# A graph network on one core: the decoder's first layer in split passes of 512 nodes, and a new order of edge blocks 0 and 1

## The reference

```python
m = gelu(h_E @ m0_w + m0_b)              # h_E: 16384 x 512, m: 16384 x 256
m = gelu(m @ m1_w + m1_b)
m = gelu(m @ m2_w + m2_b)
dh = segment_sum(m, src, 512) / 30
h = layer_norm(h_V + dh, ln1_g, ln1_b)
d = gelu(h @ d0_w + d0_b)                # the decoder: 256 -> 1024
d = gelu(d @ d1_w + d1_b)                # 1024 -> 1024
h = layer_norm(h + d @ d2_w + d2_b, ln2_g, ln2_b)
```

## Time and profile before

| | before |
|---|---|
| median of 3 runs | 592.72 us (591.55 to 592.8) |
| the profiled execution, its own time | 591.97 us |
| its span, first to last instruction | 590.1 us |
| TensorE busy | 574.3 us, 97% of the span |
| VectorE, ScalarE, GpSimd busy | 462.4, 368.9, 225.0 us |

### The profile page before, as it was taken

One profiled execution on the slowest core, in us unless ns is written; L12 is line 12 of the kernel. 1 busy time (PEld: TensorE's weight loads), 2 busy tenths in 40 slices (PEclk: granted clock), 3 DMA queues, 4 the chain that ended last, 5 costly groups with the idle time before them and its releaser, 6 DMA issues.

```text
span 590.1 us, 8593 instructions
## 1 busy us (share of the span) xinstructions
PE 574.3 (97%) x3032; PEld 487.5 (83%) x3032; DVE 462.4 (78%) x791; ACT 368.9 (63%) x564; POOL 225.0 (38%) x211
## 2 busy tenths in 40 slices
PE   7989999999999999999999999999999999999995
PEld 6778888888888888888888888888888889677763
DVE  5986487878778887788998889879766566898767
ACT  6866686767778777777776678767366444211242
POOL 4075577556666543555544555530000000200111
PEclk9999999999999999999999999999999999999999
DMA  8255487295567628456553875333163304000001
GB/s 289 87 199 168 145 284 221 115 290 177 167 187 227 190 94 260 154 153 215 163 186 110 315 247 178 114 91 88 49 271 122 142 11 143 0 2 0 1 0 36
DMA packets 34504, 86.86 MB, mean 147 GB/s; under 512 B 3872, under 2 KB 23200, under 8 KB 29856
## 3 DMA queue, kind: packets, MB, share of 16 engines
q1 hardware_dynamic: 27264, 67.09, 36.3%
q0 software_dynamic: 6912, 19.10, 8.6%
q10 hardware_dynamic: 288, 0.13, 0.1%
HBM read 66.69 MB, written 19.62 MB: 146 GB/s over the span
## 4 chain that ended last, share of the span: by engine, by line
PE 84%; DVE 9%; ACT 2%; issue 2%; POOL 1%; DMA 1%; POOLq 0%; ACTq 0%
PE ps L1356 27%; PE ps L1408 10%; PE ps L1566 7%; PE ps L1414 5%; PE ps L1390 5%; PE ps L1451 5%; PE ps L1386 5%; PE ps L1385 4%; PE ps L1528 4%; PE ps L1607 2%; PE ps L1453 2%; PE ps L1663 1%; PE ps L1578 1%; PE ps L1597 1%; PE ps L1480 1%
## 5 line engine op out<-in xcount | busy, mean ns | idle before, releaser
L497 POOL DMA_INDIRECT sorted_rows<-m,place x120 | 166.9, 1391 | 151.7 <-ACT m L560 123.7
L543 ACT ACTIVATE m_hi<-ps,cols 128x512 fp32r<-128x512 f32 x128 | 88.6, 692 | 66.8 <-PE ps L1356 41.6
L877 DVE TENSOR_TENSOR m_lo<-m_out,m_hi 128x512 fp32r<-128x512 f32 x128 | 88.6, 694 | 50.9 <-ACT m_out L545 48.0
L1356 PE MATMUL ps<-x_hi,w_hi 128*128 128x512 f32 x248 | 97.1, 391 | 0.5 <-DVE x_lo L751 0.5
L1356 PE MATMUL ps<-x_lo,w_hi 128*128 128x512 f32 x248 | 97.0, 391 | 0.0
L1356 PE MATMUL ps<-x_hi,w_lo 128*128 128x512 f32 x248 | 96.7, 390 | 0.0
L545 ACT ACTIVATE m_out<-ps,cols 128x512 f32<-128x512 f32 x128 | 88.5, 691 | 1.7 <-DVE m_lo L877 1.7
L751 DVE TENSOR_TENSOR x_lo<-x_raw,x_hi 128x1024 fp32r<-128x1024 f32 x62 | 73.1, 1219 | 5.3 <-ACT x_hi L537 5.3
L1408 PE MATMUL ps<-w_lo,m_hi 128*128 128x256 f32 x256 | 64.2, 283 | 0.0
L1408 PE MATMUL ps<-w_hi,m_hi 128*128 128x256 f32 x256 | 64.0, 282 | 0.0
L560 ACT ACTIVATE m<-m_in 128x512 f32<-128x512 f32 x64 | 39.5, 635 | 38.0 <-DVE m_in L890 38.0
(11 more groups left out here) (231 smaller groups left out, 1137.1 us busy)
## 6 DMA issues: line engine op xcount, KB each, us to landing
x_raw<-in_edges_dram SPq DMA_DIRECT2D x31, 1024.0 KB, 6.2
sorted_raw<-sorted_rows SPq DMA_DIRECT2D x24, 647.5 KB, 4.7
sorted_raw<-sorted_rows SPq DMA_DIRECT2D x6, 518.0 KB, 4.1
d_w<-in_d_dram SPq DMA_DIRECT2D x3, 1024.0 KB, 8.9
d_w<-in_d_dram SPq DMA_DIRECT2D x1, 3072.0 KB, 10.0
rows<-in_rows_dram SPq DMA_DIRECT2D x1, 2176.0 KB, 10.1
sorted_rows<-m,place POOLq DMA_INDIRECT x120, 4.8
w_raw<-in_w_dram SPq DMA_DIRECT2D x4, 256.0 KB, 5.8
```

What stands on the lines that cost most here:

```text
L497: pool.indirect_dma_start(out=sorted_d, out_offset=bass.IndirectOffsetOnAxis(ap=place[:, at:at + 1], axis=0), in_=m2[:, b % 2, t], in_offs ...
L543: nc.scalar.activation(out_hi[:, m], ps[:, bank], ACT.Gelu, bias=col(bias, m)).then_inc(hi_signal, 1)
L877: nc.vector.tensor_tensor(lo[:, m], m_out[:, m], hi[:, m].bitcast(F32), ALU.subtract).then_inc(done, 1)
L1356: last = nc.tensor.matmul(out, left, right, start=(k == 0 and i == 0), stop=(k == KE - 1 and i == 2))
```

## The change

**Edge stage.** `keep_warm` ahead of the first layer issues 7 products and not 10. `layer_0_first` takes both output halves (m = 0, 1) of a pass before the next pass, waits for high parts first and for low parts only ahead of the third pass. `layer_0(1, 0)` does the two passes with the high part of the input for all four k, then the third pass. On VectorE `rest_1(1, 0)` and `rest_1(1, 1)` go ahead of `rest_x(3)`.

**Decoder.** `d0_w` is split (`d0w_hi` by ScalarE, `d0w_lo` by VectorE, in the place of `d0_w`), and so are its inputs (`first_hi` by ScalarE from the turned columns, `first_lo` by VectorE in `first_rest`, which recomputes the plain value). There are 11 units: m = 0 to 2 for each half of 256 nodes, m = 3 to 7 for all 512. Third passes of the first and of the second three units come together, behind filler products. `d2_w` is loaded ahead of the GRU's weights.

**GRU.** For the last chunk the products of `w_hh` come before those of `w_ih`, into a bank of their own (`LAST_IN`), and VectorE's first candidate step waits for them alone.

```diff
@@ -252,7 +268,12 @@
...
         GRU_BANKS = (0, 4, 6, 0)
+        LAST_IN = 2
         NODE_HALF = (range(0, NC // 2), range(NC // 2, NC))
+        D0_HALVED = 3
+        D0_UNITS = ([(m, slice(half * N // 2, (half + 1) * N // 2)) for half in range(2) for m in range(D0_HALVED)]
+                    + [(m, slice(0, N)) for m in range(D0_HALVED, KD)])
+        UNITS = len(D0_UNITS)
...
@@ -433,10 +457,10 @@
...
             sp.dma_start(d1_w[:, D1_FIRST:].rearrange("p a b -> p (a b)"), d1_d[:, D1_FIRST * D:]).then_inc(d1_loaded, 16)
+            sp.wait_ge(d0_done, UNITS)
+            sp.dma_start(d2_w, d2_d.rearrange("p (a b) -> p a b", b=H)).then_inc(d2_loaded, 16)
...
                 sp.dma_start(dst[:].rearrange("p a b -> p (a b)"), src).then_inc(gru_loaded, 16)
-            sp.wait_ge(d0_done, 2 * KD)
-            sp.dma_start(d2_w, d2_d.rearrange("p (a b) -> p a b", b=H)).then_inc(d2_loaded, 16)
...
@@ -633,6 +657,8 @@
...
                 round_sorted(q)
+            act.wait_ge(early_loaded, 48)
+            nc.scalar.activation(d0w_hi[:], d0_w[:], ACT.Copy).then_inc(d0w_hi_done, 1)
...
@@ -663,21 +689,27 @@
...
-            act.wait_ge(early_loaded, 48)
-            affine(0, "ln1_g", "ln1_b")
+            def first_columns(half):
...
+                turned[0] += 1
+                act.wait_ge(hat_turned, turned[0])
+                for k in range(KH):
+                    nc.scalar.activation(first_hi[:, k, HALF[half]], turned_bank(half, k), ACT.Identity,
+                                         bias=col("ln1_b", k), scale=col("ln1_g", k)).then_inc(first_hi_done, 1)
...
+            first_columns(0)
             counts_out(COUNTS - 1)
-            for i in range(2 * KD):
-                half, m = divmod(i, KD)
+            for i, (m, nodes) in enumerate(D0_UNITS):
                 if i == 2:
-                    affine(1, "ln1_g", "ln1_b")
-                if i in (8, 11):
+                    first_columns(1)
+                if i in (7, 9):
                     act.wait_ge(d1_loaded, 16)
-                    round_d1w(i // 11)
+                    round_d1w(i // 9)
                 act.wait_ge(d0_done, i + 1)
-                gelu_split_out(i, ps[:, D0_BANK[m % 4], 0:NH], col("d0_b", m), d0_hi[:, m, HALF[half]])
+                gelu_split_out(i, ps[:, D0_BANK[i % 4], 0:nodes.stop - nodes.start], col("d0_b", m), d0_hi[:, m, nodes])
...
                 act.wait_ge(d1_done, m + 1)
-                gelu_split_out(2 * KD + m, ps[:, D1_BANK[m % 4]], col("d1_b", m), d1_hi[:, m])
+                gelu_split_out(UNITS + m, ps[:, D1_BANK[m % 4]], col("d1_b", m), d1_hi[:, m])
...
@@ -966,18 +998,23 @@
...
                 q = b - LAG_PREP
+                if b == 1:
+                    rest_1(1, 0)
+                    rest_1(1, 1)
...
                         add_counts(s, (b - first) // 2, (b - first) % 2)
-                rest_1(b, 0)
+                if b != 1:
+                    rest_1(b, 0)
...
                     hot_dst(q, 0)
-                rest_1(b, 1)
+                if b != 1:
+                    rest_1(b, 1)
...
@@ -1030,6 +1067,8 @@
...
             rest_direct(DIRECT[1], 1)
+            dve.wait_ge(d0w_hi_done, 1)
+            nc.vector.tensor_tensor(d0w_lo[:], d0_w[:], d0w_hi[:].bitcast(F32), ALU.subtract).then_inc(d0w_split, 1)
...
@@ -1107,6 +1146,17 @@
...
+            def first_rest(half):
...
+                dve.wait_ge(first_hi_done, KH * (half + 1))
+                for k in range(KH):
+                    nc.vector.tensor_scalar(act_T[:, k, HALF[half]], turned_bank(half, k), col("ln1_g", k), col("ln1_b", k),
+                                            ALU.mult, ALU.add).then_inc(first_plain, 1)
+                dve.wait_ge(first_plain, KH * (half + 1))
+                part = (slice(None), slice(None), HALF[half])
+                nc.vector.tensor_tensor(first_lo[part], act_T[part], first_hi[part].bitcast(F32),
+                                        ALU.subtract).then_inc(first_split, 1)
...
@@ -1127,19 +1177,23 @@
...
                 link(last)
-                moments(NODE_HALF[half])
+                variance(NODE_HALF[half])
+                if half:
+                    first_rest(0)
+                dve.wait_ge(rstd_ready, norms[0])
                 hats_written(half, lambda c: normed(res, hat, c))
-            for i in range(2 * KD):
-                half, m = divmod(i, KD)
-                rest_gelu(i, NH, d0_hi[:, m, HALF[half]], d0_lo[:, m, HALF[half]])
-                if i in (10, 12):
-                    rest_d1w(i // 12)
-                if i in (3, 5, 7, 13):
-                    piece = (3, 5, 7, 13).index(i)
+            for i, (m, nodes) in enumerate(D0_UNITS):
+                rest_gelu(i, nodes.stop - nodes.start, d0_hi[:, m, nodes], d0_lo[:, m, nodes])
+                if i == 0:
+                    first_rest(1)
+                if i in (7, 9):
+                    rest_d1w(i // 9)
+                if i in (2, 4, 5, 8):
+                    piece = (2, 4, 5, 8).index(i)
...
             for m in range(KD):
-                rest_gelu(2 * KD + m, N, d1_hi[:, m], d1_lo[:, m])
+                rest_gelu(UNITS + m, N, d1_hi[:, m], d1_lo[:, m])
...
@@ -1308,10 +1362,16 @@
...
+                bank = GRU_BANKS[c] + 1
+                hidden, inputs = ps[:, bank, H:2 * H], ps[:, bank, 0:H]
+                if c == NC - 1:
+                    hidden, inputs = ps[:, bank, 0:H], ps[:, LAST_IN, 0:H]
+                    dve.wait_ge(last_hidden, 1)
+                else:
+                    dve.wait_ge(gru_done, c + 1)
+                link(nc.vector.tensor_tensor(cand[:, c], hidden, rz[:, c, 0:H], ALU.mult))
                 dve.wait_ge(gru_done, c + 1)
-                bank = GRU_BANKS[c] + 1
-                link(nc.vector.tensor_tensor(cand[:, c], ps[:, bank, H:2 * H], rz[:, c, 0:H], ALU.mult))
-                nc.vector.tensor_tensor(cand[:, c], cand[:, c], ps[:, bank, 0:H], ALU.add).then_inc(cand_ready, 1)
+                nc.vector.tensor_tensor(cand[:, c], cand[:, c], inputs, ALU.add).then_inc(cand_ready, 1)
...
@@ -1348,6 +1408,18 @@
...
                 out = ps[:, (1, bank_x(b - 1))[m]]
+                if b == 1 and m == 0:
+                    for k in range(KE):
+                        if k % 2 == 0:
+                            pe.wait_ge(x_hi_done, 2 * b + k // 2 + 1)
+                        for part in (w_hi, w_lo):
+                            nc.tensor.matmul(out, w(0, k, m, part), x_hi[:, 1, k], start=(k == 0 and part is w_hi), stop=False)
+                    for k in range(KE):
+                        if k % 2 == 0:
+                            pe.wait_ge(x_lo_done, 2 * b + k // 2 + 1)
+                        last = nc.tensor.matmul(out, w(0, k, m, w_hi), x_lo[:, 1, k], start=False, stop=(k == KE - 1))
+                    last.then_inc(l0_done, 1)
+                    return
...
@@ -1480,7 +1560,7 @@
...
             pe.wait_ge(ident_ready, 1)
-            keep_warm(10, 0)
+            keep_warm(7, 0)
...
@@ -1518,7 +1598,7 @@
...
                 acts[0] += KH
-                return acts[0]
+                return acts[0] - 2 * KH
...
@@ -1541,37 +1621,53 @@
...
             keep_warm(2, 0)
-            turned = [turn_rows(hat, 0), None]
+            turn_rows(hat, 0)
             keep_warm(4, 0)
-            for i in range(2 * KD):
-                half, m = divmod(i, KD)
+            pe.wait_ge(d0w_split, 1)
+            for i, (m, nodes) in enumerate(D0_UNITS):
                 if i == 2:
-                    turned[1] = turn_rows(hat, 1)
-                if m == 0:
-                    pe.wait_ge(act_ready, turned[half])
+                    turn_rows(hat, 1)
...
                     pe.wait_ge(gelu_out, i - 3)
-                to_columns(d0_w, KH, m, act_T, half, ps[:, D0_BANK[m % 4], 0:NH]).then_inc(d0_done, 1)
+                out = ps[:, D0_BANK[i % 4], 0:nodes.stop - nodes.start]
+                for part in (d0w_hi, d0w_lo):
+                    for k in range(KH):
+                        if part is d0w_hi and i in (0, D0_HALVED):
+                            pe.wait_ge(first_hi_done, KH * (i // D0_HALVED) + k + 1)
+                        nc.tensor.matmul(out, part[:, k, m * P:(m + 1) * P], first_hi[:, k, nodes],
+                                         start=(k == 0 and part is d0w_hi), stop=False)
+                if i < 2 * D0_HALVED and i % D0_HALVED < D0_HALVED - 1:
+                    continue
+                if i < 2 * D0_HALVED:
+                    keep_warm(2 if i < D0_HALVED else 4, 7 if i < D0_HALVED else 2)
+                    pe.wait_ge(first_split, i // D0_HALVED + 1)
+                for u in range(i - D0_HALVED + 1 if i < 2 * D0_HALVED else i, i + 1):
+                    part_m, part_nodes = D0_UNITS[u]
+                    out = ps[:, D0_BANK[u % 4], 0:part_nodes.stop - part_nodes.start]
+                    for k in range(KH):
```

(63 more changed lines are left out.)

## The result

| | before | after |
|---|---|---|
| median of 12 runs each | 592.22 us (591.51 to 592.9) | 592.95 us (592.17 to 595.14) |
| the profiled execution | 591.97 us, span 590.1 | 592.93 us, span 591.1 |

The ratio is 1.0016, 95% interval [1.0009, 1.0024]: slower by some 0.9 us. That is clear of the noise, but even the upper end is barely over 0.2%. The forecast was 592.9. One execution of run 6 (638.08 us, mean granted clock 0.851) and one of run 7 (718.21 us, 0.753) ran in a slower state of the chip: they are in those two medians (591.42 and 592.66 us without them) and in no ratio. Two parts of the change pull against each other, and the profile has each at its place.

A forecast was written before the change was run, and what follows sets the result against it. TensorE was taken as the bound, carrying 84% of the chain of waits. Opening and block 1 -2.14, decoder +2.3 and last chunk +0.05 sum to +0.2 us, 592.9 us on the median; range 589.5 to 594.5.

The forecast's parts named there:

- The total: Whole kernel: the three terms sum to +0.2 us, giving 592.9 us on the median.
- two pauses in the decoder: Decoder's first layer: TensorE waits 1.2 us for hat of half 1 and 1.7 us for the columns of half 1.
- The opening: First microseconds: seven fillers instead of ten bring layer 1 of block 0 from 13.56 to 13.2, 0.35 us.
- Block 1: Low parts come earlier on VectorE, removing TensorE's 1.54 us wait and 0.25 restart; -2.14 us together with the opening.
- Rival 2: Block 1: VectorE stays behind, two biased and rest_0(2, 0) arriving after 36.96; 594.0 us, chance 0.12.
- The decoder: Decoder's first layer: queue-order waits and d1w_split make D1 start at 450.3 instead of 448.00, +2.3 us.
- D1 some 16.5 us after the first product: Decoder, a sign to look for: D1 starts 16.5 us after the decoder's first product instead of 14.2.
- Rival 1: Decoder: TensorE stays the bound and neither pause is seen; decoder -0.9, time 589.7 us, chance 0.34.
- my bound of -0.9: Decoder's first layer, lower bound of its term: TensorE never waits and D1 starts at 447.1.
- Rival 3: Decoder: the clock falls, products at half rate cost about 1.5 us more; 594.4 us, chance 0.08.
- the row of block 1: Block 1 before: a 1.54 us pause at granted clock 1.00, read as showing the decoder's pauses wouldn't slow the clock.

The follow-up runs named there:

- run 6: Changed kernel with the decoder's transposes of half 1 moved behind fillers and third passes of units 0 to 2: 591.44 us, ratio 0.9985 to the kernel before.
- run 7: Changed kernel with more filler products ahead of the transposes and of unit 3, so TensorE never rests in the decoder's pauses: 592.69 us, ratio 1.0010 to before.
- run 1: Kernel before with the edge stage's part alone (opening and VectorE's order in block 1): 590.10 us, ratio 0.9962.
- run 8: Changed kernel without the 12 filler records inside the decoder's units: 592.77 us, ratio 1.0006 to the kernel before.
- run 9: Changed kernel with the transposes of half 1 ahead of unit 3 and ScalarE's columns behind the first Gelu: 590.63 us, ratio 0.9973 to the kernel before.
- run 5: Changed kernel with ScalarE's first_columns(1) moved ahead of the Gelus of units 0 and 1: 591.12 us, ratio 0.9978 to the kernel before.
- run 10: Changed kernel without the decoder's 12 filler records and with ScalarE's columns of half 1 one unit later: 593.54 us, ratio 1.0016 to the kernel before.
- Run 3: Kernel before with the opening alone (seven fillers, new pass order in layer_0_first and layer_0(1, 0)): 591.99 us, ratio 0.9992.
- run 4: Kernel before with the decoder's part alone (split d0 weights, 11 units, third passes behind fillers, d2_w earlier): 596.56 us, ratio 1.0069.

## Why the prediction was right

**The total** came out as forecast (592.95 against 592.9), and that is in part luck: as a change +0.2 was forecast and +0.7 to +0.9 measured. Two terms were off by 0.39 and 0.34 us, both to the slow side (the profiled execution was forecast at 592.2 and took 592.93), and that it isn't seen in the median is because before's median was 592.72 over the 3 runs shown and is 592.22 over 12. What did hold is the mechanism: a gain in block 1, two pauses in the decoder that eat it, each where it was forecast.

**The opening** was the mis-sized term, 0.35 us for layer 1 of block 0 (13.2); after's trace shows 13.63, later than before's 13.56. It was reckoned for a clock that rises at the moment of before, 7.85. Run 1 has that case: its second pair of products takes 0.57 us, between the 0.85 of the low level and 0.46, so the rise comes at some 7.8, and layer 1 starts at 13.48. That is 0.08 us gained, not 0.35. Two steps of the sum were too kind. The last product of the layer moves by 0.53 us (12.45 against 12.98) where 0.7 was forecast, since the first two take 1.02 and not 0.86 and start at 6.53, not 6.4; and ending second to last and not fourth to last costs two products, 0.45 us, where the sum has 0.37. The rest is the condition. After's second pair takes 0.78 us, so its rise is near 8.2; in runs 8 and 9 the pair from 7.36 and 7.37 is fast already and layer 1 starts at 13.17 and 13.21; in runs 5 and 10 three pairs are slow, to 9.16, and it starts at 14.12 and 14.15. The forecast's 13.2 was reached only where the clock rose earlier than it had assumed. The Trainium skill (TensorE: Matmul & The Clock Gate, What you observe) says that the moment of the first rise varies between runs, and these traces agree (some 7.8 us in run 1, 8.2 in after). Run 3's 0.5 us has no counterpart in any of them, and its interval holds zero.

**Block 1** was right in mechanism and place: the 1.54 us and the restart went (1.75 us measured, 1.79 forecast without the opening's 0.35), VectorE's queue kept up, and no wait opened between there and the decoder. Rival 2 is out: run 1 shows the gain whole.

**The decoder**, +2.3 forecast, +2.64 measured. The waits were forecast at 1.2 and 1.7 us and are 1.12 and 1.64, and D1 is set by `d1w_split`, as the sum had it. Moved by the 1.75 us of block 1 into the times of the forecast, after's first Gelu starts at 437.90 (forecast 437.75), unit 3's at 443.17 (442.88) and D1 at 450.64 (450.3). So 0.15 of the 0.34 us is there by the first Gelu and 0.29 by unit 3's, in several steps of some 0.1 us each and with no single place; a full unit also takes 1.39 us (441.69 to 443.09) and not 1.36, but that isn't on the path that ended last. The chain to `d1w_split` itself was added up 0.2 us too high: its terms give 450.1, not 450.3. The sign "D1 some 16.5 us after the first product" failed, with 17.26: 0.34 of it is the later D1, and the rest comes from a first product that starts 0.45 us earlier than in before's order (433.38 in those times, not 433.83), since it waits for one slice of columns, with nothing gained by it behind.

Rival 1 (no pauses) is out in after. Run 9, with 0.65 us of waiting left, comes nearest to it: D1 after 14.98 us, where my bound of -0.9 had 13.3. The bound had no place for ScalarE's queue up to `d1w_split`, which run 9 meets 7.47 us after unit 3's Gelu as after does.

**Rival 3**, the fallen clock, is real, which the row of block 1 had made me hold unlikely. It isn't in after's profile (granted clock 1.00 throughout the decoder), but two of after's twelve runs took 595.0 and 595.1 us at a mean clock of 0.994, the others 592.2 to 594.4 at 0.997 to 0.998. That in those two the clock fell in the decoder is inferred from runs 8 and 10, not seen. Its price was forecast at 1.5 us, which its own terms don't give (18 products at 0.12 and half a unit of 1.36, each once more, are 2.8); run 10 shows 1.5 us of work lost and 0.88 at D1. What stays open is why four of run 4's five executions have the low mean clock and only two of after's twelve, with the same pauses in both, and what makes the rest of the 2 us by which those four are slower.

**The best version** measured is the edge stage alone, 590.10 us, 0.38% under before; run 9 with both parts (590.63) isn't told apart from it. No experiment gave a decoder that earns its change. Run 9 without the fillers ahead of its second third passes (437.34 to 438.15, while `first_lo` is ready at 437.64) wasn't tried.

## What to carry to other kernels

Fewer columns to stream gain nothing where the next operand stands behind other work in an in-order queue: write down for each new wait what its producer has ahead of it in its own queue, and move the producer up before splitting the product. Filler products ahead of a late operand don't bring it sooner, and where the operand is nearly there they cost time themselves (0.87 us, run 8 against after); what they seem to guard is the clock, whose fall cost 0.88 us at D1 in the execution that shows it. And an edit that puts products into the first microseconds earns half of what it seems or less, since they run there at the low clock for a time that differs between executions: in run 1 the first product is 1.14 us ahead and the last of the layer 0.53. One profile can't judge such an edit, for the same opening gave 13.17 and 14.15.

## What was unexpected of the hardware

In run 10's profiled execution rests of 1.11 and 2.36 us, with less than 2 us of work between them, were followed by 3.4 us at a granted clock of 0.50, while the single one of 1.54 us in block 1 before stood in a stretch of 1.00, and run 8's profiled execution, with 1.11 and 1.64, stays at 1.00 throughout the decoder. And the granted clock's column doesn't tell all: in run 9 it reads 1.00 from 0 to 20 us, though the 14 fillers from 3.45 to 6.51 take 0.22 us each and the eight from 437.34 to 438.15 only 0.10.
